# Attention between images: mask by a TensorE product, softmax on compact logits, value means by products

## The reference

```python
q, k, v = conv3x3(x, Wq), conv3x3(x, Wk), conv3x3(x, Wv)
att = jnp.einsum('nchw,mchw->nmhw', q, k) / jnp.sqrt(jnp.float32(C))
att = jax.nn.softmax(att, axis=1)
virt = jnp.einsum('nmhw,mchw->nchw', att, v)
mu = jnp.mean(virt, axis=(1, 2, 3), keepdims=True)
var = jnp.var(virt, axis=(1, 2, 3), keepdims=True)
virt = (virt - mu) * jax.lax.rsqrt(var + 1e-05)
virt = virt * gamma[None, :, None, None] + beta[None, :, None, None]
virt = jax.nn.relu(virt)
virt = conv3x3(virt, Wc)
return x + virt
```

## Time and profile before

| | us |
|---|---|
| median of 3 runs | 523.4 (523.14 to 523.52) |
| the profiled execution's own time | 525.22 |
| its span in the trace | 523.4 |
| TensorE busy | 476.1 (91%) |
| VectorE (DVE) busy | 353.3 (68%) |
| ScalarE (ACT) busy | 263.9 (50%) |
| GpSimd (POOL) busy | 136.6 (26%) |

### The profile page before, as it was taken

The page is one execution under the profiler, slowest core; times in us unless marked ns, Lnnn a source line. Parts: engine busy times, 40 slices in busy tenths (PEclk is TensorE's granted clock), DMA queues, the critical chain, the costliest instruction groups (busy, mean ns, idle before and its releaser), DMA issues.

```text
span 523.4 us, 10554 instructions
## 1 busy us (share of the span) xinstructions
PE 476.1 (91%) x3746; PEld 377.3 (72%) x3746; DVE 353.3 (68%) x895; ACT 263.9 (50%) x654; POOL 136.6 (26%) x161
## 2 busy tenths in 40 slices
PE   8698899989999999999999999989988998785895
PEld 7575766668687767767776877667676788785885
DVE  1628737895778678686967777784467345675995
ACT  4235466664646454555546464443534514984540
POOL 5320663261013102210410221030110012504662
PEclk9999869999999999999999999998997999997999
DMA  5000111000000000000000000000000000004111
GB/s 219 21 20 3 45 46 43 24 21 23 0 21 22 1 0 20 20 0 0 20 20 0 20 0 0 2 22 0 1 7 15 1 22 1 1 0 162 43 59 61
DMA packets 9488, 13.18 MB, mean 25 GB/s; under 512 B 496, under 2 KB 8816, under 8 KB 9328
## 3 DMA queue, kind: packets, MB, share of 16 engines
q1 hardware_dynamic: 9456, 12.76, 7.3%
HBM read 8.56 MB, written 4.19 MB: 24 GB/s over the span
## 4 chain that ended last, share of the span: by engine, by line
PE 60%; DVE 23%; issue 8%; ACT 7%; DVEq 1%; POOL 0%; ACTq 0%
PE bank L1202 7%; PE bank L1403 5%; PE bank L1204 5%; PE bank L1203 5%; PE bank L1321 5%; PE bank L1377 4%; PE bank L1209 3%; DVE nmax L995 3%; PE bank L1353 2%; PE bank L1375 2%; PE bank L1390 2%; PE bank L1431 2%; ACT x L801 2%; PE bank L1226 2%; DVE even L895 2%
## 5 line engine op out<-in xcount | busy, mean ns | idle before, releaser
L1202 PE MATMUL bank<-win,w_hi 128*128 128x256 f32 x384 | 121.4, 316 | 12.7 <-DVE win L1148 5.9
L1203 PE MATMUL bank<-win,w_hi 128*128 128x256 f32 x384 | 108.8, 283 | 0.0
L1204 PE MATMUL bank<-win,w_lo 128*128 128x256 f32 x384 | 108.8, 283 | 0.0
L743 ACT ACTIVATE prob<-bank 128x512 f32<-128x512 f32 x128 | 69.6, 597 | 76.1 <-PE bank L1375 75.3
L995 DVE TENSOR_REDUCE nmax<-bank 128x2 f32<-128x512 f32 x128 | 85.4, 685 | 27.9 <-PE bank L1353 27.3
L1202 PEld LDWEIGHTS bank<-win,w_hi 128*128 128x128 f32 x384 | 73.3, 191 | 24.0 <-issue 11.2
L1203 PEld LDWEIGHTS bank<-win,w_hi 128*128 128x128 f32 x384 | 73.5, 191 | 0.5
L1204 PEld LDWEIGHTS bank<-win,w_lo 128*128 128x128 f32 x384 | 73.2, 191 | 0.0
L520 POOL TENSOR_TENSOR first<-first 128x256 f32<-128x256 f32 x24 | 17.8, 740 | 167.6 <-ACT first L632 167.6
L1377 PE MATMUL bank<-qk 32*128 32x256 f32 x256 | 41.6, 341 | 3.0 <-ACT prob L743 2.6
L1209 PE MATMUL bank<-ones_r 128*128 128x256 f32 x224 | 39.8, 318 | 1.1 <-DVE ones_r L849 1.1
(11 more groups left out here) (237 smaller groups left out, 933.9 us busy)
## 6 DMA issues: line engine op xcount, KB each, us to landing
w_stage<-convs SPq DMA_DIRECT2D x4, 576.0 KB, 3.8
x_in<-x SPq DMA_DIRECT2D x8, 256.0 KB, 2.7
out<-x_pair SPq DMA_DIRECT2D x8, 256.0 KB, 2.2
q<-out SPq DMA_DIRECT2D x1, 2048.0 KB, 8.3
out<-v SPq DMA_DIRECT2D x8, 256.0 KB, 2.1
cst<-small SPq DMA_DIRECT2D x1, 1708.0 KB, 8.3
cst<-small SPq DMA_DIRECT2D x1, 253.5 KB, 2.9
```

Of the source, the lines that this page charges most:

```text
L743: act.activation(prob[:, x // 4 % 2, x % 4, :, :], bank[ST_BANK[x % 2]][:, :], ACT.Exp, scale=L2_SCALE).then_inc(st_exp, 1)
L1202: mm(dst, hi, x_hi, start=(row == 0), stop=False)
L1203: mm(dst, hi, x_lo, start=False, stop=False)
L1204: return mm(dst, lo, x_hi, start=False, stop=(row == KH - 1))
```

## The change

L3's stage is rewritten; nothing before it and nothing after the normalization's variance changes.

1. `logits3`: the mask is written into the bank by one product of the identity and the mask (F32R, 128 x 512), and the four logit products accumulate on it. ACT prepares the two F32R constants beforehand (two 128 x 128 copies).
2. `row3`: one DVE reduction of the bank (maximum over 8 columns at a time) takes out 64 values for each row of a batch. With only one unmasked entry in 8, that maximum is the entry: c3 holds 32 tiles x 16 = 512 compact logits for each partition.
3. The softmax runs on c3 in two halves (4 batches, 256 columns each): DVE maximum and subtraction (`shift3`), ACT one exponential with the scale in it, DVE sum, reciprocal and multiplication (`norm3`).
4. POOL spreads a batch of the compact weights to 128 x 512 by multiplying them with `pixel3` (0 or 1); both operands are read with repeated elements.
5. Pair 7's convolution: group 4 is issued before the logits, group 5 between batches 3 and 4 (before: in twos between the batches).
6. One loop holds the rest. v3_t has room for all batches; its copies out of PSUM are ACT's for even and DVE's for odd batches. `join(PAIRS - 1, 2)` stands after norm3(0) in DVE's queue.
7. The mean of the values comes from four products of `mean_all` with virt, for each batch, accumulated in bank 0 (128 columns); only the squares still go through DVE's sum over pixels and a product (bank 1, 16 columns). At the end DVE reduces the 128 columns to 16 and copies the 16 of the squares.

```diff
...
+        c3 = x1[:, :, :].rearrange("p m x -> p (m x)")
+        small3 = ab_sq[:, :, :].rearrange("p r f -> p (r f)").rearrange("p (k t) -> p k t", t=HW // GPX)
+        max3, att3_sum, att3_inv = small3[:, 0, :], small3[:, 1, :], small3[:, 2, :]
+        ident_r, mask3_r = q_max[:, 0, 0:P], q_max[:, 0, P:2 * P]
...
+        v3_t = prob_flat.rearrange("p (b g c) -> p b g c", g=BATCH, c=C)
...
+            for w in range(3):
                 first_sum(PAIRS - 1, w)
 
             for b in range(BATCHES):
...
+                pool.wait_ge(att3_normed, b // (BATCHES // 2) + 1)
                 if b >= 2:
                     pool.wait_ge(att3t_done, b - 1)
...
+                pool.tensor_tensor(att3_n[b % 2].rearrange("p (t n x) -> p (t n) x", n=N, x=GPX),
+                                   c3[:, b * BATCH * N:(b + 1) * BATCH * N].unsqueeze(2).to_broadcast([P, BATCH * N, GPX]),
+                                   c("pixel3").unsqueeze(1).to_broadcast([P, BATCH * N, GPX]),
+                                   ALU.mult).then_inc(att3_spread, 1)
...
+            act.activation(ident_r, c("ident"), ACT.Copy).then_inc(mask3_ready, 1)
+            act.activation(mask3_r, c("mask3"), ACT.Copy).then_inc(mask3_ready, 1)
+            for w in range(3):
+                first_copy(PAIRS - 1, w)
+
             def v3t_copy(b):
                 act.wait_ge(v3t_done, b + 1)
...
+                act.activation(v3_t[:, b, :, :], bank[2 + b % 2][:, :], ACT.Copy).then_inc(v3t_by_act, 1)
+
+            def exponentials(h):
+                act.wait_ge(soft3_chain, 4 * h + 2)
+                b = h * BATCHES // 2
+                act.activation(compact(b, BATCHES // 2), compact(b, BATCHES // 2), ACT.Exp,
+                               scale=L3_SCALE).then_inc(att3_exp, 1)
+
+            exponentials(0)
+            v3t_copy(0)
+            exponentials(1)
+            for b in range(BATCHES + 1):
                 if b < BATCHES:
...
+                    act.wait_ge(att3t_done, b + 1)
+                    act.activation(att3_t[:, batch(b)], bank[4 + b % 2][:, :], ACT.Copy).then_inc(att3t_copied, 1)
+                if b + 2 < BATCHES and b % 2 == 0:
+                    v3t_copy(b + 2)
+                a = b - 1
                 if a >= 0:
...
                     act.wait_ge(virt_done, a + 1)
                     if a >= 2:
...
+                        act.wait_ge(sum3_done, a - 1)
...
+            def row3(b):
+                dve.wait_ge(dot3_done, b + 1)
+                dve.tensor_reduce(c3[:, b * BATCH * N:(b + 1) * BATCH * N],
+                                  bank[b % 2][:, :].rearrange("p (k x) -> p k x", x=GPX), X, ALU.max).then_inc(row3_done, 1)
+
+            def shift3(h):
+                b = h * BATCHES // 2
+                part, cols = compact(b, BATCHES // 2), half3(h)
+                dve.wait_ge(row3_done, b + BATCHES // 2)
+                dve.tensor_reduce(max3[:, cols], part, X, ALU.max).then_inc(soft3_chain, 1)
+                dve.wait_ge(soft3_chain, 4 * h + 1)
+                dve.tensor_tensor(part, part, max3[:, cols].unsqueeze(2).to_broadcast([P, BATCHES // 2 * BATCH, N]),
+                                  ALU.subtract).then_inc(soft3_chain, 1)
+
+            def norm3(h):
+                part, cols = compact(h * BATCHES // 2, BATCHES // 2), half3(h)
+                dve.wait_ge(att3_exp, h + 1)
+                dve.tensor_reduce(att3_sum[:, cols], part, X, ALU.add).then_inc(soft3_chain, 1)
+                dve.wait_ge(soft3_chain, 4 * h + 3)
+                dve.reciprocal(att3_inv[:, cols], att3_sum[:, cols]).then_inc(soft3_chain, 1)
+                dve.wait_ge(soft3_chain, 4 * h + 4)
+                dve.tensor_tensor(part, part, att3_inv[:, cols].unsqueeze(2).to_broadcast([P, BATCHES // 2 * BATCH, N]),
+                                  ALU.mult).then_inc(att3_normed, 1)
+
+            def v3t_copy(b):
+                dve.wait_ge(v3t_done, b + 1)
+                dve.tensor_copy(v3_t[:, b, :, :].rearrange("p g c -> p (g c)"), bank[2 + b % 2][:, :]).then_inc(v3t_by_dve, 1)
+
+            def sum_squares(b):
                 if b >= 2:
                     dve.wait_ge(tot3_done, b - 1)
...
+                dve.wait_ge(sq3_done, b + 1)
+                dve.tensor_reduce(sum3[:, b % 2, :], sq3[b % 2].rearrange("p (g n x) -> p n g x", n=N, x=GPX), XY,
+                                  ALU.add).then_inc(sum3_done, 1)
+
+            dve.wait_ge(pv_done, 2 * QUADS * PAIRS)
+            for b in range(4):
+                row3(b)
+            shift3(0)
+            row3(4)
+            row3(5)
+            norm3(0)
+            join(PAIRS - 1, 2)
+            row3(6)
+            row3(7)
+            shift3(1)
+            v3t_copy(1)
+            norm3(1)
+            v3t_copy(3)
+            sum_squares(0)
+            v3t_copy(5)
+            sum_squares(1)
+            v3t_copy(7)
+            for b in range(2, BATCHES):
+                sum_squares(b)
             dve.wait_ge(tot3_done, BATCHES)
...
+            dve.tensor_reduce(tmv3[:, 0, :], bank[0][:, 0:P].rearrange("p (n x) -> p n x", x=GPX), X, ALU.add).then_inc(ln_chain, 1)
+            dve.tensor_copy(tmv3[:, 1, :], bank[1][:, 0:N]).then_inc(ln_chain, 1)
...
+            convolve(PAIRS - 1, 4 * UNITS, 5 * UNITS)
+            pe.wait_ge(mask3_ready, 2)
             pe.wait_ge(x3_done, 2 * PAIRS)
             q3, k3, v3 = qkv3
 
             def tile(b, g):
                 return slice((b * BATCH + g) * P, (b * BATCH + g + 1) * P)
+
+            def logits3(b):
+                if b >= 2:
+                    pe.wait_ge(row3_done, b - 1)
+                mm(bank[b % 2][:, :], ident_r, mask3_r.unsqueeze(1).to_broadcast([P, BATCH, P]), start=True, stop=False)
+                if b == 0:
+                    pe.wait_ge(joined, 3 * PAIRS - 1)
+                for g in range(BATCH):
+                    ins = mm(bank[b % 2][:, g * P:(g + 1) * P], q3[:, tile(b, g)], k3[:, tile(b, g)],
+                             start=False, stop=(g == BATCH - 1))
+                ins.then_inc(dot3_done, 1)
+
+            def v3t_copied(b):
+                pe.wait_ge(v3t_by_dve if b % 2 else v3t_by_act, b // 2 + 1)
 
             def v3_transposed(b):
                 if b == 0:
                     pe.wait_ge(joined, 3 * PAIRS)
                 if b >= 2:
...
+                    v3t_copied(b - 2)
                 for g in range(BATCH):
                     ins = tr(bank[2 + b % 2][:, g * C:(g + 1) * C], v3[:, tile(b, g)], ident)
                 ins.then_inc(v3t_done, 1)
 
+            def att3_transposed(a):
+                pe.wait_ge(att3_spread, a + 1)
+                if a >= 2:
+                    pe.wait_ge(att3t_copied, a - 1)
+                for g in range(BATCH):
+                    ins = tr(bank[4 + a % 2][:, g * P:(g + 1) * P], att3_n[a % 2][:, g * P:(g + 1) * P], ident)
+                ins.then_inc(att3t_done, 1)
+
             def attended(a):
                 pe.wait_ge(att3t_copied, a + 1)
...
+                v3t_copied(a)
                 if a >= 2:
                     pe.wait_ge(sq3_done, a - 1)
                 for g in range(BATCH):
...
+                    ins = mm(bank[6 + a % 2][:, g * P:(g + 1) * P], v3_t[:, a, g, :], att3_t[:, tile(a, g)],
                              start=True, stop=True)
                 ins.then_inc(virt_done, 1)
 
...
+            def mean_values(a):
+                pe.wait_ge(virt_copied, a + 1)
+                for g in range(BATCH):
+                    mm(bank[0][:, 0:P], c("mean_all"), virt[:, tile(a, g)], start=(a == 0 and g == 0),
+                       stop=(a == BATCHES - 1 and g == BATCH - 1))
+
+            def mean_squares(a):
+                pe.wait_ge(sum3_done, a + 1)
+                mm(bank[1][:, 0:N], c("mean_all"), sum3[:, a % 2, :], start=(a == 0),
+                   stop=(a == BATCHES - 1)).then_inc(tot3_done, 1)
+
+            for b in range(4):
+                logits3(b)
+            convolve(PAIRS - 1, 5 * UNITS, 6 * UNITS)
+            for b in range(4, BATCHES):
+                logits3(b)
+            v3_transposed(0)
+            v3_transposed(1)
+            pe.wait_ge(row3_done, BATCHES)
+            for b in range(BATCHES + 4):
                 if b < BATCHES:
...
+                    att3_transposed(b)
+                if b + 2 < BATCHES:
+                    v3_transposed(b + 2)
+                if 0 <= b - 1 < BATCHES:
                     attended(b - 1)
...
+                if 0 <= b - 2 < BATCHES:
+                    mean_values(b - 2)
+                if 0 <= b - 4 < BATCHES:
+                    mean_squares(b - 4)
...
+    t["pixel3"] = np.where(r[:, None] % GPX == np.arange(GPX)[None, :], 1.0, 0.0)
```

More of the change, by code:

```diff
@@ L270, in program @@
         y = qkv3[2]
-        sum3 = sb("sum3", [P, 2, 2, N])
+        sum3 = sb("sum3", [P, 2, N])
         tm3 = sb("tm3", [P, N])
@@ L795, in _ @@
-            for b in range(BATCHES + 2):
-                if b < BATCHES:
```

(33 more changed lines are left out.)

94 lines of the change are left out of this document (13 added, 81 removed).

## The result

The changed kernel takes 527.09 us (median of 5 runs, 526.66 to 528.09), the kernel before 523.4; the ratio of record is 1.0058 (95% interval 1.0036 to 1.0080), a little less than the 1.0071 of the two medians. Measured again beside other kernels on one chip it was 1.0051 (1.0033 to 1.0069). The forecast was 525.9 with a range of 524.5 to 527.5 and 0.88 for slower. The time lies in that range, but 0.3 above the narrower 525.2 to 526.8 that I had given 0.62.

What follows compares the result with a forecast made beforehand. ACT paced the stage's first half and PE filled the second; in the new loop PE alone binds. +2.3 us to the stage's end and +0.25 after it, on the 523.4 median, gave 525.9 us, range 524.5 to 527.5.

Steps and rivals of the forecast that it cites:

- Bound: L3's stage before: ACT's L801 paces the first half, about 2.0 us a batch; PE fills the second's 1.50 us period.
- the removal of L801: First half of L3's stage: replacing ACT's 64 short instructions by two exponentials removes 18.6 us of ACT work.
- Start and logits: Before the loop: group 4 fills PE's wait, logits end at 448.9 us, PE idles 1.4, loop begins at 451.2.
- The loop: Weights, values and means: PE alone binds at 2.82 us a batch, against 1.50 before; last DVE sum ends at 474.35.
- the stall of 0.2: Loop's start: shift3(1), a v copy and exponential 1 delay PE's second v transpose and first `attended` by 0.2 us.
- the tail: After the last `attended`: mean_values 6 and 7 and mean_squares 4 and 5 take PE 2.08 us, to 472.8.
- After the stage: DVE reduces 128 columns and copies 16, 0.35 + 0.12 instead of 0.23: +0.25 us; nothing added for PE's lower clock.
- Sum: Whole kernel: span 523.4 + 2.3 + 0.25 = 525.95 us; the same 2.5 on the median gives 525.9.
- the first rival: Longer middle: a POOL spread holds shift3(1), then exponential 1 and the first att3t copy, up to 1.55 us; 527.4; chance 0.16.
- POOL: Edit 4's spread: 1.04 us, at most 1.55, hidden because PE afterwards asks for one in 2.8 us.
- The rule weighed: VectorE and GpSimd share a port pair held for a whole instruction, so shift3(1) could wait for a spread's rest.
- Faster, if `mean_values` ran at the F32R rate: Loop: 0.06 us per 128-column product, 0.24 a batch, 5.3 less, 520.6; faster only if four cost under 0.5; chance 0.05.

Runs made afterwards that it cites:

- the experiment with group 4 first: The kernel before with only group 4 of the last pair's convolution issued before the logits; stage 45.58 us against 44.98, ratio 0.9990.
- The experiment with two spreads: The changed kernel with every spread on POOL done twice; stage 49.15 us against 46.99, one run.
- the kernel with the early join: The changed kernel with join(PAIRS - 1, 2) moved ahead of the fifth row maximum in DVE's queue; stage 46.46 us against 46.99, ratio to before 1.0057.
- the F32R kernel: The changed kernel with a batch's four fp32 mean products made one F32R product of 512 columns; stage 42.19 us against 46.99, ratio to before 0.9971.

## Why the prediction was right

**Bound.** That the first half had PE idle to win and the second had nothing to spare held. Edits 1 to 6 gained 2.3 us, edit 7 lost 4.3 to 4.9. From 463 to 469 us in the kernel before PE was busy for 5.94 of 6 us and ACT for 6.00, so both were full there. That the first half was ACT's is shown by the experiment with group 4 first, where PE's filled wait gained nothing. One reading was too high: the removal of L801 does not free 18.6 us of ACT. The accumulator's records overlap the exponentials beside them (a pair starts every 0.39 us), so the 32 pairs took about 12.4 us, and ACT's busy time from 437 to 472 us fell by 12.6. The sum did not use the 18.6.

**Start and logits.** PE had no idle before group 4. The loop's start was forecast at 451.2 - 427.08 = 24.1 us into the stage, and is at 23.83. PE's wait before the loop, 1.4 forecast, was 0.79 + 0.34 = 1.1 by its weight loads. Most of the 0.3 are small steps on DVE: norm3(0) took 0.99 in place of 1.08, the two last row maxima 1.21 in place of 1.32.

**The loop.** Forecast 451.2 to 474.35, 23.15 us; measured 23.16. A batch was 2.66 rather than the 2.82 that I wrote, since the mean product's 0.14 was in it from the fifth iteration only, as was counted in the sum; the sum, not the batch, was the forecast. The agreement is not an accident of terms that cancel: by the weight loads the last `attended` ends 19.53 us after the loop's start (19.5 forecast, with the stall of 0.2, which is there), the tail is 2.1 (2.08), and from it to the read of the means it is 1.5 (1.57). `mean_values` has its 64 records and 0.89.

**After the stage.** This term was sized too high: +0.25 forecast, 0.09 measured. The reduction of 128 columns took 0.29, not 0.35, and the copy behind it was nearly hidden. From the read of the means to the end of the span it is 51.46 us and was 51.34 before, so that nothing had to be added for the clock at its lower level held.

**Sum.** +2.3 + 0.25 = 2.55 was forecast for the span; by the stage and the step after it it is 2.01 + 0.09 = 2.1, to which the ratios 1.0058 and 1.0051 (3.0 and 2.7 us, each at least 0.9 us uncertain) fit. The median given, 527.09, is 1.2 above the forecast and 1.6 above what these 2.1 give (525.5). The traced stage does not hold that difference. A drift ahead of it, in either kernel's executions, would explain it, but no run here shows that. The account holds for the stage; that the whole time stayed in the range, whose upper end is 0.4 away, is in part luck. It also lies 0.3 from the 527.4 of the first rival, whose mechanism is absent: its longer middle would stand in the stage. The profiled pair's spans differ by only 1.9, since the changed one's stage began 0.23 earlier.

**POOL.** Hidden, with 1.14 a spread. The experiment with two spreads shows that the margin is smaller than I argued: in the first three iterations PE asks for spreads faster than once in 2.8 us.

**The rule weighed.** The contention is real here and cost the changed kernel nothing. norm3(1)'s multiplication (L1117) has a mean of 0.820 in two instances; the timeline has 0.42 for the first, with POOL idle, and 1.22 for the second, beside a spread:

```profile
452.58 1.15 POOL L575 TENSOR_TENSOR xn<-x,cst 128x512 f32<-128x512 f32 x1
...
452.79 1.22 DVE L1117 TENSOR_TENSOR x<-x,ab_sq 128x256 f32<-128x256 f32 x1
```

It did not hold PE up, since POOL needs norm3(1) only for the fifth batch's spread, and PE through it. shift3(1), which I had named, was free (0.43), and was held (0.90) in the kernel with the early join, where it goes with the 0.35 us by which the stage gained less than the loop's start. Neither row has L1171's small surcharge of 0.21. What each got longer goes with what was left of the spread when it started: 0.80 us longer with 0.94 left (452.79 to 453.73), 0.48 longer with 0.62 left (448.00 to 448.62). That agrees with the Trainium skill, page SBUF — State Buffer, section SBUF: two separate sides, by which the port pair is held for a whole instruction.

**The rival that was nearest to a way out.** "Faster, if `mean_values` ran at the F32R rate" was rightly put aside for this kernel, and is close to what the F32R kernel brings about with one product of 512 columns: 4.80 us less in the stage, where 5.3 was written. Its rate for 128 columns was wrong, though: 0.10 a product, not 0.06. Its turning point was off as well: 2.55 us over eight batches are 0.32 each, so four products had to cost under 0.58, not 0.5, to make the change a gain.

## What to carry to other kernels

Before moving a reduction onto TensorE, read the period of one batch in the stage where it will run, and add up PE's instructions in it: here 0.14 + 0.47 + 0.89 was the whole period, and 0.89 more of fp32 products went almost whole into the time, while DVE, busy for 23.1 of 35 us, had room for the same sums. Judge the parts of a large change one by one; here a rewrite that gained 2.3 us carried one edit that lost 4.3, and taking that edit back gave 0.993 to 0.995 of the old time. And when executions drift by more than the effect, measure a stage between two instants of the trace that bracket the edit, not the whole span.

## What I had not expected of the hardware

Four F32R products of 128 columns with the same stationary operand take 0.40 us and one of 512 columns 0.23, so a product of 128 columns costs 0.10 and not a quarter of 0.23. Whether its weight load sets that was not tested. A POOL and a DVE instruction that both read SBUF can stretch a DVE operation of 0.42 us to 1.22, and POOL's spread from 1.14 to 1.32 (1.22 in the changed kernel, 1.32 in the one with the early join). The part of the program ahead of the stage, the same in all kernels but for two or three small copies on ACT, ended anywhere from 420.8 to 427.2 us. In two traces of the changed kernel that goes with TensorE's granted clock; for the rest it is open.
